# Two layers of graph network on one core: fp32 messages summed unsplit, counting merged with the first sort passes, node stages cut finer

## The chip, the cores and the metric

The kernel runs on one core of one Trainium2 chip. The metric is the device time of one execution in microseconds. One launch computes everything.

## What is computed

N = 6250 nodes with 64 features, E = 200,000 directed edges sorted by `dst`, 64 features per edge. Two layers, each on a normalized `x` and each added back to `x`:

```python
h = relu(layernorm(x))
# layer 1: attention over both directions of every edge
gl, gr = (h @ Wl.T)[src], (h @ Wr.T)[dst]           # src, dst: 2 E entries, 4 heads of 16
score = (att * leaky_relu(gl + gr, 0.2)).sum(-1)
alpha = softmax of score over the entries of one src
out = segment_sum(gr * alpha, src)                  # 6250 x 64
x = x + gelu(concat(out, h) @ W1.T + b1) @ W2.T + b2
# layer 2: plain messages
h = relu(layernorm(x))
agg = segment_sum(h[src] + edge_attr_64, dst)       # 6250 x 64
y = relu(agg @ W1 + b1) @ W2 + b2
x = x + batchnorm(y) * gamma + beta
```

Everything is fp32. `src` and `dst` are drawn at random, so each row of `h[src]` is fetched by its index.

## The kernel before, in words

The nodes lie in 49 blocks of 128 (a partition each). Seven stages follow one another, each a block of five instruction lists with a barrier of all engines behind it.

1. `prepare`: first layernorm, the tables `gl_table` and `gr_table` in HBM, and one sort key per entry (block and node numbers in 26 bits, carried as fp32), 3136 of the 4096 columns of `keys`. How many keys lie below each block boundary is counted 49 times over all 3136 columns: 28 times by VectorE (L431), 21 times by ScalarE (L332, sign with a running sum). From the counts come the padding keys in the columns from 3072 on, which make every block's share a multiple of 256. Both engines write the counting's waste into `keys[1]`.
2. `sort`: a bitonic sort of 128 x 4096 keys. Stages 1 to 11 work within runs along a partition: 66 passes over the whole array, of four instructions of 1024 elements each (`one_pass_by_runs`, L538 to L541). Then eight stages that cross partitions, with transposes on TensorE (L610) and copies back on ScalarE (L619). GpSimd's only part is an iota, `bits` (L519), for which the first VectorE instruction waits (L550).
3. `decode`: VectorE unpacks keys into rows and places. The row numbers to gather, `row_of` (L700), are the last but three of its instructions.
4. `attention`: 403 steps of 1024 entries in 13 chunks. GpSimd issues eight indirect gathers of 128 rows a step (L815), in eight slots; VectorE makes one-hots (L970, L1002) and scans scores, TensorE multiplies.
5. `attention_nodes`: dividing by the softmax's sums (`share` L1248, `mixed` L1251), then 13 rounds of at most four blocks on TensorE and ScalarE; VectorE adds each round to `x` (L1259), and when all are in, does the layernorm over all 49 blocks (five operations over 3136 columns); a store of `h2_table` ends it. GpSimd makes `nodes` by an iota, clears `agg`, and copies `dst_f` meanwhile.
6. `messages`: 98 groups of 2048 edges, 196 halves of eight tiles of 128. For each half GpSimd issues eight gathers (L1308) into one of six slots. VectorE adds the edge rows into PSUM (L1384), makes a bf16 one-hot of `dst` (L1358), and together with ScalarE splits the message in three bf16 parts (L1387, L1391), which TensorE sums by one-hots (L1329) in one matmul of 192 columns per tile. A group whose edges span more than one block of nodes takes a step more for each further block, with a one-hot of all 16 tiles made of two SBUF operands, `nodes` and `dst_f` (48 such steps in all).
7. `message_nodes`: the three parts of `agg` are added over all blocks (L1508, L1509), then matmuls, batch norm and the store.

A buffer is reused when the last reader has signalled. The order on each engine is the order in which the code is written; no planner is at work. GpSimd's gathers of a half wait for `s_message` of the half six before.

## Time and profile before

| | us |
|---|---|
| median of 3 runs | 7588.72 (7580.87 to 7643.47) |
| the profiled execution | 7608.22 |
| its span | 7606.3 |
| prepare, to the first pass of the sort | 0 to 172 |
| 66 passes within runs | 172 to 483 |
| crossing stages of the sort | 483 to 1095 |
| decode | 1095 to 1134 |
| attention, gathers | 1134 to 5225 |
| attention's end (last scan and sums) | 5225 to 5371 |
| attention_nodes | 5371 to 5461 |
| messages, gathers | 5461 to 7522 |
| last sums and message_nodes | 7522 to 7606 |

The page's first part gives each engine's busy time over the whole span. Since the stages have different limits, these shares say little of any one stage. The groups by line tell how long an engine was idle just ahead of an instruction, and what ended it. A timeline row is one instruction, or several alike. Idle time that stands before a gather as "issue" is the pause that GpSimd makes between two of them.

### The profile page before, as it was taken

What the parts mean: (1) busy time and instruction counts of PE and PEld (TensorE: products, weight loads), DVE (VectorE), ACT (ScalarE), POOL (GpSimd) and SP (SyncE); (2) the same over time, 40 slices, a digit from 0 to 9 for tenths busy, and PEclk for the clock granted to TensorE, in tenths of its full rate; (3) what the DMA queues carried; (4) which work ended last, traced back from release to release, by engine and by line L of the source; (5) the groups of instructions that cost most, each with busy time, mean ns of one, the idle gap of its engine ahead of it and who ended that gap; (6) DMA issues with size and microseconds to landing.
All of it is one profiled execution on the core that took longest, in us unless ns stands there. A gap on an engine that the chain in (4) does not pass through costs nothing. (4 is left out here: it accounts for less than half of the span.)

```text
span 7606.3 us, 71089 instructions
## 1 busy us (share of the span) xinstructions
PE 3570.6 (47%) x16583; PEld 3314.3 (44%) x16583; DVE 4721.4 (62%) x7539; ACT 733.2 (10%) x1147; POOL 4711.1 (62%) x4809
## 2 busy tenths in 40 slices
PE   2001114476776767677677776767411112222224
PEld 1001114466666767676676666767311111111112
DVE  8999993567676776767667676777433333333443
ACT  4001100000000000000000000000111111111111
POOL 0000007777777777777777777773277777777774
PEclk9995555555555555555555555555655555555555
DMA  2000004344443444444444443442122221111111
GB/s 35 0 0 0 0 20 103 103 120 118 116 118 103 135 115 120 118 113 121 111 127 115 117 122 100 135 112 83 44 51 53 51 51 50 50 50 50 49 47 29
DMA packets 631893, 600.13 MB, mean 79 GB/s; under 512 B 382418, under 2 KB 385618, under 8 KB 631206
## 3 DMA queue, kind: packets, MB, share of 16 engines
q10 hardware_dynamic: 177888, 320.64, 12.9%
q0 software_dynamic: 153344, 157.33, 10.4%
q1 hardware_dynamic: 300230, 117.47, 5.9%
q8 instruction: 142, 2.33, 0.1%
q14 instruction: 289, 2.37, 0.1%
HBM read 480.76 MB, written 114.19 MB: 78 GB/s over the span
## 5 line engine op out<-in xcount | busy, mean ns | idle before, releaser
L815 POOL DMA_INDIRECT rows<-gr_table,row_of x3224 | 3109.2, 964 | 1946.2 <-issue 1945.0
L1308 POOL DMA_INDIRECT message<-h_table,src_sb x1568 | 1582.8, 1009 | 552.7 <-issue 477.6
L846 PE MATMUL bank<-terms,hot_sum 128*128 128x68 f32 x6448 | 1468.3, 423 | 777.8 <-DVE acc L981 774.2
L846 PEld LDWEIGHTS bank<-terms,hot_sum 128*128 128x128 f32 x6448 | 1409.4, 331 | 826.2 <-DVE hot_sum L1002 820.1
L836 PE MATMUL bank<-gl_step,hot_t 128*128 128x64 f32 x6448 | 1459.1, 421 | 282.4 <-DVE hot_t L970 240.6
L836 PEld LDWEIGHTS bank<-gl_step,hot_t 128*128 128x128 f32 x6448 | 1421.6, 333 | 293.7 <-DVE hot_t L970 290.6
L1329 PE MATMUL bank<-edge_parts,edge_hot 128*128 128x192 bf16 x1568 | 286.3, 364 | 1597.0 <-DVE edge_parts L1391 1597.0
L1022 DVE TENSOR_TENSOR fore<-bank,rows 128x512 f32<-128x512 f32 x403 | 277.7, 689 | 1083.3 <-DMA rows<-gr_table,row_of 1083.3
L1329 PEld LDWEIGHTS bank<-edge_parts,edge_hot 128*128 128x128 bf16 x1568 | 202.6, 140 | 1680.5 <-DVE edge_parts L1391 1669.4
L1384 DVE TENSOR_TENSOR bank<-message,edge 128x512 f32<-128x512 f32 x196 | 142.0, 724 | 1007.1 <-DMA message<-h_table,src_sb 1007.1
L952 ACT ACTIVATE bank<-fore 128x512 f32<-128x512 f32 x403 | 242.4, 602 | 3383.6 <-DVE fore L1022 3383.6
L1002 DVE TENSOR_TENSOR hot_sum<-bank,place 128x1024 f32<-128x1024 f32 x403 | 490.6, 1217 | 0.0
L970 DVE TENSOR_TENSOR hot_t<-place_b,bank 128x1024 f32<-128x1024 bf16 x403 | 489.2, 1214 | 0.7 <-DMA place_b<-place_rows 0.7
L981 DVE TENSOR_TENSOR acc<-acc,bank 128x68 f32 x1612 | 354.2, 220 | 182.9 <-DVE acc L981 133.9
L610 PE MATMUL bank<-ident,keys 128*128 128x128 f32 x448 | 96.8, 406 | 787.3 <-DVEq L596 698.8
L610 PEld LDWEIGHTS bank<-ident,keys 128*128 128x128 f32 x448 | 87.1, 217 | 797.8 <-DVEq L596 704.9
L138 DVE TENSOR_REDUCE scores<-top 128x32 f32<-128x512 f32 x403 | 276.3, 686 | 59.5 <-DVE top L1039 1.5
L1028 DVE TENSOR_TENSOR fore<-fore,bank 128x512 f32<-128x512 f32 x403 | 274.5, 681 | 21.3 <-ACT bank L952 21.3
L530 DVE TENSOR_TENSOR keys<-keys 128x1024 f32<-128x1024 f32 (+1 forms) x166 | 275.9, 1662 | 7.9 <-ACT keys L619 2.0
L995 DVE TENSOR_TENSOR terms<-rows_again,bank 128x512 f32<-128x512 f32 x403 | 273.2, 678 | 4.3
L531 DVE TENSOR_TENSOR keys<-keys 128x1024 f32<-128x1024 f32 (+1 forms) x166 | 274.8, 1655 | 0.0
L1039 DVE TENSOR_TENSOR top<-fore,bank 128x512 f32<-128x512 f32 x403 | 273.8, 679 | 0.0
(264 smaller groups left out, 2867.6 us busy)
## 6 DMA issues: line engine op xcount, KB each, us to landing
place_b<-place_rows ACTq DMA_DIRECT2D x403, 256.0 KB, 3.6
gr_rows<-rows ACTq DMA_DIRECT2D x403, 256.0 KB, 2.0
rows_again<-gr_rows ACTq DMA_DIRECT2D x403, 256.0 KB
rows<-gr_table,row_of POOLq DMA_INDIRECT x3224
gl_step<-gl_table SPq DMA_DIRECT2D x1612, 32.0 KB
edge<-in_edge_attr SPq DMA_DIRECT2D x97, 512.0 KB, 3.6
message<-h_table,src_sb POOLq DMA_INDIRECT x1568, 2.4
pen_s<-pen_rows ACTq DMA_DIRECT2D x52, 64.0 KB, 2.0
```

What stands on the lines that cost most here:

```text
L138: return dve.tensor_reduce(out, in_, AX.X, op)
L530: dve.tensor_tensor(vb[:, 0], va[:, 0], va[:, 1], ALU.min)
L531: c.link(dve.tensor_tensor(vb[:, 1], va[:, 0], va[:, 1], ALU.max))
L815: pool.indirect_dma_start(rows[k][:, g, :], None, m.gr_table[:, :], bass.IndirectOffsetOnAxis(m.row_of[:, tile:tile + 1], 0)).then_inc(s_g ...
L836: last = pe.matmul(bank[q % LAG][:, g * D:(g + 1) * D], hot_t[q % LAG][:, g * P:(g + 1) * P], gl_s[q % U][:, g // GROUP_TILES, :], start=T ...
L846: last = pe.matmul(sums_of(r % SUM_SLOTS, g // GROUP_TILES), hot2[r % LAG][:, g, :], by_tile[:, g, :], start=g % GROUP_TILES == 0, stop=g ...
L970: dve.tensor_tensor(hot_t[q % LAG][:, :], place_b[q % V][:, :], node_ps.to_broadcast([P, STEP]), ALU.is_equal).then_inc(s_hot, 1)
L981: dve.tensor_tensor(sums, sums, sums_of(r % SUM_SLOTS, i), ALU.add).then_inc(s_acc, 1)
L1002: dve.tensor_tensor(hot2[r % LAG][:, :, :], places, at, ALU.is_equal).then_inc(s_summed, 1)
L1022: dve.tensor_tensor(z[:, :, :], left_of(q % LAG), rows[q % U][:, :, :], ALU.add).then_inc(s_z, 1)
L1308: pool.indirect_dma_start(rows[k][:, e, :], None, m.h2_table[:, :], bass.IndirectOffsetOnAxis(m.src[:, tile:tile + 1], 0)).then_inc(s_gath ...
L1329: done = pe.matmul(out[:, 0:3 * D], one_hot[:, e, :], parts[h % 4][:, e, :, :].rearrange("p w f -> p (w f)"), start=first and e == 0, stop ...
```

## The change

Six edits:

- **Messages.** ScalarE copies the edge attributes into PSUM, VectorE adds the gathered rows to them into SBUF as fp32, and TensorE sums with fp32 one-hots, 64 columns per tile. No splitting; `agg` is one part, not three. One-hots of the next group are made once this group's messages are. The further one-hot reads its node numbers from PSUM, where a copy of 128 columns puts them.
- **Counting and sorting.** ScalarE does all 49 counts. Meanwhile VectorE runs the sort's stages 1 to 9 on columns 0 to 3071 and stage 10 on the first half; the rest is done once the padding keys stand. `sort` has no block of its own any more; its iota is the second instruction of GpSimd's list.
- **Early gathers.** `row_of` is computed ahead of nine other instructions of `decode`, and GpSimd issues the gathers of the first four steps (32 of 3224) inside `decode`.
- **attention_nodes.** GpSimd's iota, clearing and copy wait for `mixed`. `mixed` is made in two pieces (8 and 41 blocks). The layernorm's mean, difference, square and sum are taken round by round. The last operation and the store are in two pieces (24 and 25 blocks).
- **message_nodes.** The two additions over `agg` are gone.

```diff
-            for b in range(VECTOR_COUNTS, BLOCKS):
-                at_least(act, s_cnt_act, b - VECTOR_COUNTS)
-                nc.scalar.activation(junk_act, src_f[:, :], ACT.Sign, bias=bias[:, b:b + 1],
+            for b in range(BLOCKS):
+                at_least(act, s_cnt_act, b)
+                nc.scalar.activation(junk[:, :], src_f[:, :], ACT.Sign, bias=bias[:, b:b + 1],
                                      accum_out=below[:, b:b + 1]).then_inc(s_cnt_act, 1)
+            sort.scalar(act)
...
+            dve.wait_ge(s_cnt_act, BLOCKS)
+            c.link(dve.tensor_scalar(below[:, :], below[:, :], -0.5, float(EDGE_COLS), ALU.mult, ALU.add))
+            dve.engine_nop().then_inc(s_cnt, 1)
...
+    def vector_front(self, dve):
+        self.c = Chain(dve, self.s_chain)
+        self.stages(dve, 1, self.FRONT_STAGES - 1, 0, self.FRONT)
+        self.stages(dve, self.FRONT_STAGES, self.FRONT_STAGES, 0, ROW // 2)
...
+        self.stages(dve, 1, 7, self.FRONT, self.PADS)
+        self.stages(dve, 8, self.FRONT_STAGES - 1, self.FRONT, ROW - self.FRONT)
+        self.stages(dve, self.FRONT_STAGES, self.FRONT_STAGES, ROW // 2, ROW // 2)
+        self.stages(dve, self.FRONT_STAGES + 1, LOG_ROW - 1, 0, ROW)
```

```diff
+        @block.gpsimd
+        def _(pool):
+            pool.wait_ge(s_row, 1)
+            for q in range(EARLY):
+                for g in range(STEP_TILES):
+                    tile = q * STEP_TILES + g
+                    pool.indirect_dma_start(m.rows[q][:, g, :], None, m.gr_table[:, :],
+                                            bass.IndirectOffsetOnAxis(m.row_of[:, tile:tile + 1], 0)
+                                            ).then_inc(m.s_gath[q], 16)
...
+            dve.wait_ge(s_moved, 8)
+            c.link(dve.tensor_scalar(pad_row[:, :], m.iota_node[:, 0:1], float(BLOCKS * P), None, ALU.add))
+            c.link(dve.tensor_single_scalar(pad_t[:, :], key_t[:, :].bitcast(I32), NODE_MASK, ALU.bitwise_and))
+            dve.tensor_scalar(m.row_of[:, :], pad_t[:, :], pad_row[:, :], None, ALU.min).then_inc(s_row, 1)
...
-            for q in range(STEPS):
+            for q in range(EARLY, STEPS):
```

```diff
+            pool.wait_ge(s_mixed, 2)
...
-                dve.tensor_tensor(m.x[:, b:b + n, :], m.x[:, b:b + n, :],
-                                  bank[4 + r % 2][:, 0:n * D].rearrange("p (b f) -> p b f", f=D), ALU.add
+                x, h, square = (tile[:, b:b + n, :] for tile in (m.x, m.h, mixed))
...
-            layernorm_steps(m, chain, dve, m.x, m.h, mixed, s_var, s_std, 1).then_inc(s_h2, 1)
+                dve.wait_ge(s_add, r + 1)
+                chain.link(nc_reduce(dve, mean, x))
+                chain.link(dve.tensor_scalar(mean, mean, 1.0 / D, None, ALU.mult))
+                chain.link(dve.tensor_tensor(h, x, mean.unsqueeze(2).to_broadcast([P, n, D]), ALU.subtract))
+                chain.link(dve.tensor_tensor(square, h, h, ALU.mult))
+                chain.link(nc_reduce(dve, var, square))
+            dve.tensor_scalar(m.var[:, :], m.var[:, :], 1.0 / D, LN_EPS, ALU.mult, ALU.add).then_inc(s_var, 1)
+            dve.wait_ge(s_std, 1)
+            chain.link(dve.reciprocal(m.rstd[:, :], m.rstd[:, :]))
+            chain.link(dve.tensor_tensor(m.mean[:, :], m.rstd[:, :], m.rstd[:, :], ALU.mult))
+            chain.link(dve.tensor_tensor(m.mean[:, :], m.mean[:, :], m.var[:, :], ALU.mult))
...
+            chain.link(dve.tensor_tensor(m.rstd[:, :], m.rstd[:, :], m.mean[:, :], ALU.mult))
+            for lo, hi in ((0, FRONT), (FRONT, BLOCKS)):
+                h = m.h[:, lo:hi, :]
+                dve.scalar_tensor_tensor(h, h, 0.0, m.rstd[:, lo:hi].unsqueeze(2).to_broadcast([P, hi - lo, D]), ALU.max,
+                                         ALU.mult).then_inc(s_h2, 1)
```

```diff
-    hot = [sb(f"edge_hot{k}", [P, HALF, P], BF16, ctx) for k in range(4)]
-    hot_more = sb("edge_hot_more", [P, 2, HALF, P], BF16, ctx)
-    parts = [sb(f"edge_parts{k}", [P, HALF, 3, D], BF16, ctx) for k in range(4)]
+    rows = [sb(f"edge_rows{k}", [P, HALF, D], F32, ctx) for k in range(U)]
+    edge = [sb(f"edge{k}", [P, 2, HALF, D], F32, ctx) for k in range(W)]
+    messages_s = [sb(f"message{k}", [P, 2, HALF, D], F32, ctx) for k in range(V)]
+    hot = [sb(f"edge_hot{k}", [P, HALF, P], F32, ctx) for k in range(4)]
+    hot_more = sb("edge_hot_more", [P, EDGE_TILES, P], F32, ctx)
+    numbers_ps, past_ps = (bank[3][:, i * P:(i + 1) * P] for i in range(2))
...
-            def scatter(out, one_hot, h, first, last):
+            def scatter(out, one_hot, g, way, first, last):
                 for e in range(HALF):
-                    done = pe.matmul(out[:, 0:3 * D], one_hot[:, e, :], parts[h % 4][:, e, :, :].rearrange("p w f -> p (w f)"),
...
             for h in range(HALVES):
-                act.wait_ge(s_message, h + 1)
-                nc.scalar.copy(parts[h % 4][:, :, 0, :], message_of(h)).then_inc(s_hi, 1)
-                act.wait_ge(s_rest, h + 1)
-                nc.scalar.copy(parts[h % 4][:, :, 1, :], message_of(h)).then_inc(s_mid, 1)
+                g, way = h // 2, h % 2
+                act.wait_ge(s_edge[g % W], (g // W + 1) * 16)
+                at_least(act, s_message, h - 1)
+                nc.scalar.copy(edge_ps(h), edge[g % W][:, way, :, :]).then_inc(s_edge_ps, 1)
...
+            def hot_first(g):
+                for h in (2 * g, 2 * g + 1):
+                    hot_of(hot[h % 4][:, :, :], numbers_ps, m.dst_f[:, h * HALF:(h + 1) * HALF], HALF
+                           ).then_inc(s_hot_first, 1)
...
+            hot_first(0)
             before = steps_before(dve, 0)
             for g in range(EDGE_GROUPS):
                 for way in range(2):
                     h = 2 * g + way
-                    k = h % U
-                    message, piece = message_of(h), parts[h % 4]
-                    dve.wait_ge(s_edge[g % V], (g // V + 1) * 16)
-                    dve.wait_ge(s_gath[k], (h // U + 1) * 16 * HALF)
-                    dve.tensor_tensor(message, rows[k][:, :, :], edge[g % V][:, way, :, :], ALU.add).then_inc(s_message, 1)
-                    hot_of(hot[h % 4][:, :, :], bank[3][:, 0:P], m.dst_f[:, h * HALF:(h + 1) * HALF], HALF)
-                    dve.wait_ge(s_hi, h + 1)
-                    dve.tensor_tensor(message, message, piece[:, :, 0, :], ALU.subtract).then_inc(s_rest, 1)
+                    dve.wait_ge(s_edge_ps, h + 1)
+                    dve.wait_ge(s_gath[h % U], (h // U + 1) * 16 * HALF)
+                    dve.tensor_tensor(messages_s[g % V][:, way, :, :], edge_ps(h), rows[h % U][:, :, :], ALU.add
+                                      ).then_inc(s_message, 1)
                     if g and not way:
                         add_first(g - 1, before)
-                    dve.wait_ge(s_mid, h + 1)
-                    dve.tensor_tensor(piece[:, :, 2, :], message, piece[:, :, 1, :], ALU.subtract).then_inc(s_parts, 1)
+                if g + 1 < EDGE_GROUPS:
+                    hot_first(g + 1)
...
-                        hot_of(hot_more[:, :, :, :].rearrange("p a t n -> p (a t) n"), m.nodes[:, bass.ds(past * P, P)],
-                               m.dst_f[:, g * EDGE_TILES:(g + 1) * EDGE_TILES], EDGE_TILES).then_inc(s_hot, 1)
+                        dve.tensor_copy(past_ps, m.nodes[:, bass.ds(past * P, P)]).then_inc(s_past, 1)
+                        dve.wait_ge(s_past, r + 1)
+                        hot_of(hot_more[:, :, :], past_ps, m.dst_f[:, g * EDGE_TILES:(g + 1) * EDGE_TILES], EDGE_TILES
+                               ).then_inc(s_hot, 1)
...
             c = Chain(dve, s_chain)
-            c.link(dve.tensor_tensor(m.agg[:, :, 1, :], m.agg[:, :, 1, :], m.agg[:, :, 2, :], ALU.add))
```

VectorE in `messages`, before: one half and the start of the next. `edge_parts` are the bf16 parts, `edge` the attributes, `message` the gathered rows (and, in the bank, their sum).

```order
L1384 TENSOR_TENSOR bank<-message,edge 128x512 [waits s_edge_gath2,s_edge1]
L1358 TENSOR_TENSOR edge_hot<-bank,dst_f 128x1024
L1387 TENSOR_TENSOR bank<-bank,edge_parts 128x512 [waits s_edge_hi]
L1363 TENSOR_LOAD first_of
L1363 ISA x2
L1365 REGISTER_ALU
L1367 ISA [waits s_edge_first_ps,s_agg]
L1367 TENSOR_TENSOR agg<-agg,bank 128x192
L1391 TENSOR_TENSOR edge_parts<-bank,edge_parts 128x8x64 [waits s_edge_mid]
L1384 TENSOR_TENSOR bank<-message,edge 128x512 [waits s_edge_gath3,s_edge1]
L1358 TENSOR_TENSOR edge_hot<-bank,dst_f 128x1024
L1387 TENSOR_TENSOR bank<-bank,edge_parts 128x512 [waits s_edge_hi]
```

And now, a half and the next, then the one-hots of the next group; `edge_rows` are the gathered rows.

```order
L1454 TENSOR_TENSOR message<-bank,edge_rows 128x512 [waits s_edge_gath2,s_edge_attr_ps]
L1434 TENSOR_LOAD first_of
L1434 ISA x2
L1436 REGISTER_ALU
L1438 ISA [waits s_edge_first_ps,s_agg]
L1438 TENSOR_TENSOR agg<-agg,bank 128x64
L1454 TENSOR_TENSOR message<-bank,edge_rows 128x512 [waits s_edge_gath3,s_edge_attr_ps]
L1423 TENSOR_TENSOR edge_hot<-bank,dst_f 128x1024 x2
```

The first addition had two inputs in SBUF; it has one in PSUM now. Per half two subtractions are gone, and both one-hots of a group come together behind its additions.

GpSimd from the last instruction of `prepare` to the gathers, before (the ISA without a name ahead of the iota is no arithmetic).

```order
L353 ISA spans<-span 128x196 [waits s_span]
L285 UNCONDITIONAL_BRANCH
L517 UNCONDITIONAL_BRANCH [waits barrier_Pool_Activation_PE_DVE_SP_gather]
L519 ISA
L519 IOTA bits 128x7
L516 UNCONDITIONAL_BRANCH
L806 UNCONDITIONAL_BRANCH [waits barrier_Pool_Activation_PE_DVE_SP_gather]
L815 DMA rows<-gr_table,row_of 128x64 x64
```

And now.

```order
L353 ISA spans<-span 128x196 [waits s_span]
L283 UNCONDITIONAL_BRANCH
L690 UNCONDITIONAL_BRANCH [waits barrier_Pool_Activation_PE_DVE_SP_gather]
L696 DMA rows<-gr_table,row_of 128x64 [waits s_dec_row]
L696 DMA rows<-gr_table,row_of 128x64 x31
L679 UNCONDITIONAL_BRANCH
L846 UNCONDITIONAL_BRANCH [waits barrier_Pool_Activation_PE_DVE_SP_gather]
L855 DMA rows<-gr_table,row_of 128x64 x32
```

The iota `bits` has moved to the start of `prepare`, behind the clearing of `ident`, and half of the 64 gathers in sight have moved ahead of a barrier, to where `s_dec_row` releases them.

## Rows read from the trace of the kernel before

**Rows 1.** The page's first part: busy time, share of the span, instructions of each engine.

```profile
PE 3570.6 (47%) x16583; PEld 3314.3 (44%) x16583; DVE 4721.4 (62%) x7539; ACT 733.2 (10%) x1147; POOL 4711.1 (62%) x4809
```

**Rows 2.** Groups of instructions, message stage: busy us, mean ns | idle before, releaser.

```profile
L1308 POOL DMA_INDIRECT message<-h_table,src_sb x1568 | 1582.8, 1009 | 552.7 <-issue 477.6 <-POOLq L1161 75.1
...
L1384 DVE TENSOR_TENSOR bank<-message,edge 128x512 f32<-128x512 f32 x196 | 142.0, 724 | 1007.1 <-DMA message<-h_table,src_sb 1007.1
```

**Rows 3.** One line's instructions: duration ns min/median/max, first and last start.

```profile
L815 POOL DMA_INDIRECT rows<-gr_table,row_of x3224: 940/944/2982, 1133.8 to 5224.4; - x190
L1308 POOL DMA_INDIRECT message<-h_table,src_sb x1568: 940/944/2864, 5461.2 to 7520.6; - x196
```

**Rows 4.** Timeline, message stage: start us, duration us, engine, line, operation [idle before].

```profile
6511.57 0.70 DVE L1384 TENSOR_TENSOR bank<-message,edge 128x512 f32<-128x512 f32 x1 [6.08 <-DMA message<-h_table,src_sb]
6511.67 1.41 POOL L1308 DMA_INDIRECT message<-h_table,src_sb  x1 [0.30 <-issue]
...
6516.22 2.29 DVE L1358 TENSOR_TENSOR edge_hot_more<-nodes,dst_f 128x2048 bf16<-128x2048 f32 x1 [0.87 <-issue]
...
6517.12 2.20 POOL L1308 DMA_INDIRECT message<-h_table,src_sb  x1 [0.31 <-issue]
```

**Rows 5.** Timeline, attention stage.

```profile
2502.85 1.22 DVE L1002 TENSOR_TENSOR hot_sum<-bank,place 128x1024 f32<-128x1024 f32 x1
2503.02 0.94 POOL L815 DMA_INDIRECT rows<-gr_table,row_of  x1 [0.30 <-issue]
```

**Rows 6.** Timeline, prepare and sort.

```profile
46.44 3.41 DVE L431 TENSOR_SCALAR_CACHE_REDUCE keys<-src_f 128x3136 bf16<-128x3136 f32 x1
...
80.44 2.92 ACT L332 ACTIVATE keys<-src_f,bias 128x3136 bf16<-128x3136 f32 x1
...
144.23 0.18 DVE L434 TENSOR_SCALAR below<-below 128x21 f32<-128x21 f32 x1 [0.88 <-ACT keys L332]
...
160.75 0.99 DVE L490 CAST blk_i<-blk_f 1x1612 int32<-1x1612 f32 x1
...
169.99 1.28 DVE L550 TENSOR_SCALAR bits<-bits 128x1 int32<-128x1 int32 x7 [8.25 <-POOL bits L519]
...
189.09 1.23 DVE L539 TENSOR_TENSOR keys<-keys 128x1024 f32<-128x1024 f32 x1
...
193.75 1.23 DVE L539 TENSOR_TENSOR keys<-keys 128x1024 f32<-128x1024 f32 x1
...
1042.31 0.68 DVE L581 TENSOR_TENSOR keys<-keys 128x512 f32<-128x512 f32 x1
...
1042.91 0.69 DVE L580 TENSOR_TENSOR keys<-keys 128x512 f32<-128x512 f32 x1
```

**Rows 7.** Timeline, end of decode and first gather of the attention stage.

```profile
1123.18 1.91 DVE L700 TENSOR_SCALAR row_of<-seg_i,pad_row 128x3232 int32<-128x3232 int32 x1
...
1133.75 1.29 POOL L815 DMA_INDIRECT rows<-gr_table,row_of  x1 [963.80 <-issue]
```

**Rows 8.** Busy time in one window, decode: start:end, length, busy us (instructions), PEclk, DMA share, GB/s.

```profile
1102.80:1132.50 29.70, 29.08 (x13) 0.53 0.17 71
```

**Rows 9.** Timeline, one gather while VectorE scans a chunk.

```profile
1464.88 2.37 POOL L815 DMA_INDIRECT rows<-gr_table,row_of  x1 [0.30 <-issue]
```

**Rows 10.** Timeline, node stage after attention.

```profile
5371.12 5.39 DVE L1248 TENSOR_SCALAR share<-acc 128x196 f32<-128x196 f32 x1
...
5381.44 0.42 PE L1185 MATMUL bank<-ident,mixed 128*64 128x128 f32 x1 [17.01 <-DVE mixed L1251]
...
5425.67 0.42 DVE L1259 TENSOR_TENSOR x_sb<-x_sb,bank 128x256 f32<-128x256 f32 x1 [3.46 <-PE bank L1204]
...
5431.09 3.42 DVE L138 TENSOR_REDUCE mean<-x_sb 128x49 f32<-128x3136 f32 x1
...
5461.16 2.15 POOL L1308 DMA_INDIRECT message<-h_table,src_sb  x1 [75.10 <-POOLq L1161]
```

**Rows 11.** Timeline, start of the last node stage.

```profile
7536.39 1.91 PE L1442 MATMUL bank<-ident,agg 128*64 128x128 f32 x8 [7.83 <-DVE agg L1509]
```

More of the change, by code:

```diff
@@ L194, in build @@
         m.row_of = sb("row_of", [P, TILES_UP], I32, layer0)
+        m.rows = [sb(f"rows{k}", [P, STEP_TILES, D], F32, layer0) for k in range(GATHER_SLOTS)]
+        m.s_gath = [sem(f"s_gath{k}") for k in range(GATHER_SLOTS)]
         m.keys = [sb("keys0", [P, ROW], F32, keys_ctx), sb("keys1", [P, ROW], F32, keys_ctx)]
         with ExitStack() as ctx:
-            prepare(m, ctx)
-        if stop == "prepare":
-            return m
-        with ExitStack() as ctx:
-            final = sort(m, ctx)
+            final = prepare(m, ctx, Sort(m, ctx))
         if stop == "sort":
@@ L227, in build, with prepare @@
         return m
-def prepare(m, ctx):
+def prepare(m, ctx, sort):
     nc, t, sb, sem, bank = m.nc, m.t, m.sb, m.sem, m.bank
@@ L716, in attention @@
     PAIRS = STEP_TILES * HEADS
-    rows = [sb(f"rows{k}", [P, STEP_TILES, D], F32, ctx) for k in range(U)]
+    rows = m.rows
     rows2 = [sb(f"rows_again{k}", [P, STEP_TILES, D], F32, ctx) for k in range(V)]
@@ L752, in attention @@
     s_pool = m.s_pool
[L753 removed]
+    s_gath = m.s_gath
     s_store = [sem(f"s_store{k}") for k in range(U)]
```

337 lines of the change are left out of this document (177 added, 160 removed).

## The prediction, made before the changed kernel ran

> **What bounds the kernel now.** I read the page's first part to see whether one engine fills the span. None does: TensorE 47%, VectorE and GpSimd 62% each [rows 1]. So each stage has its own limit, and I went through the stages.
>
> The two gather stages hold 6150 of 7606 us. In `messages` VectorE's addition L1384 stood idle 1007 us ahead of itself, waiting for gathered rows [rows 2]. The gathers wait for nobody: ahead of them GpSimd's idle time is "issue" (477.6 us over 1568) and the one stage change (75.1) [rows 2]. So this stage is as long as GpSimd needs to issue 1568 gathers: 2060.4 us from 5461.2 to the end of the last at 7521.5 [rows 3]. VectorE, TensorE and ScalarE there matter only by what they do to GpSimd.
>
> They do something. The median gather takes 944 ns, the mean 1009 [rows 2, 3]. The timeline shows which are the long ones: one issued just after L1384 (two inputs in SBUF) takes 1.41 us, one under L1358 with `nodes` and `dst_f` in SBUF 2.20 us; each ends about 0.8 us after the VectorE instruction does [rows 4]. In the attention stage the one-hot L1002 (one input in PSUM) runs 1.22 us and the gather beside it takes 0.94 [rows 5]. There only scans, with long instructions that read SBUF alone, hold gathers up [rows 9]. So an instruction with two SBUF inputs holds the next gather until its end, and one with an input in PSUM doesn't. The undisturbed pace is 0.944 + 0.305 (the pause, 477.6/1568) = 1.249 us.
>
> Outside the gather stages VectorE sets the pace: in `prepare` and `sort` it stands still 8.25 us for the iota `bits` [rows 6] and otherwise hardly at all.
>
> **Messages: 101 us gained.** All of VectorE's instructions over a half now have an input in PSUM: the addition, the one-hots, the sums, and the further one-hot, which gets its numbers by a copy of 128 columns. The kind of L1002 [rows 5] then holds for every one. The excess of the gathers is 1582.8 − 1568 × 0.944 = 102.6 us [rows 2, 3]; the stage becomes 1568 × 1.249 = 1958, plus 1 for its first gather (2.15 [rows 10]), so 1959 against 2060.4. Do others become the bound? A half lasts 8 × 1.249 = 10.0 us. VectorE has about 0.7 + 1.22 [rows 2, 5] and a small sum per half, 2.5 us; TensorE eight fp32 matmuls, at most 3.4 if each takes 0.42 as a 128-column one does [rows 10]; ScalarE has one copy where it had two. A further step adds 16 matmuls and 2.3 us of VectorE, 48 times in all. Six slots of rows cover that. Bounds: 80, if the SBUF to PSUM copy and other short accesses still hold some; 103, if nothing does.
>
> **Prepare and sort: 105 us gained.** VectorE gives up 28 counts, 46.44 to 144.2, about 97 us [rows 6]. Every sort pass it does ahead of the counts' end is work it must do anyway. Its price: an instruction of 1024 elements comes every 1.135 us, four make 4.66 with the pass's 0.12 [rows 6]; 512 elements take 0.60 [rows 6]. So one takes 0.07 + 1.04 ns per element. Stages 1 to 9 are 45 passes of 768: 45 × 3.6 = 162; ten passes of 512 are 25; with 2 for the start the front is 189, from 46.4 to 236. ScalarE's 49 counts at 3.04 each (21 of them fill 80.44 to 144.2) last from 80.4 to 229 [rows 6], 7 us ahead of VectorE. Behind come 21 us of small operations (as before, 144.2 to 161.7 [rows 6], with the round trips), then the pads: 28 passes of 64 elements at about 0.66, 19; stages 8 and 9 on the 1024 other columns, 17 × 1.46 = 25; stage 10 on the second half, 25; stage 11 in full, 11 × 4.66 = 51; 2 for the bits. End: 236 + 21 + 120 = 377, against 483 before (172 + 66 × 4.66 + 3). The sort itself is no shorter (309 for 311); the gain is the counts and the 8.25 us gap, whose iota now runs at the very start. That the iota costs 8 us there is hidden by the loads of `prepare`. Bounds: 85, if the small pad instructions take twice my figure (nothing as short as 64 elements with this pattern is in my rows); 108 if VectorE waits for nothing at all. ScalarE becomes the later one if a count takes over 0.14 us more than it did.
>
> **Early gathers: 9 us gained.** Now the first gather starts at 1133.75, behind the block's end [rows 7]; the 33rd comes 32 × 1.249 = 40 us later, 1173.7. In the changed order `row_of` is ready after the three moved instructions, at 1106.9 in the old times, and VectorE's other nine end at 1132.1: the 29.1 us busy of the window less the 3.9 of the moved ones is 25.2 [rows 8]. Several have two SBUF inputs. For those that have one (tensor_scalar over 4096 columns) no gather of before shows what they do. If all eight long ones hold a gather each, 8 are out at 1132.1, and 24 × 1.249 = 30 later all 32; with 1.4 for the stage change the 33rd starts at 1163.5: 10 gained. If none holds, it starts at 1148.4: 25 gained. I take 9, nearest the first end, since a scan's instructions hold gathers for 2.37 us too [rows 9]. The low end is 0: the barrier behind `decode` must now wait for GpSimd, and a start-up of 7 to 8 us on GpSimd, like the gap ahead of `bits`, could lie before the first.
>
> Here the Trainium skill speaks: "SBUF — State Buffer" says that `tensor_scalar` with fp32 in SBUF can enter a mode that takes the port pair shared with GpSimd, for the whole instruction. By that rule the gain would be 10, without it up to 25; no trace here shows it.
>
> **attention_nodes: 19 us gained.** `share` takes 5.39 us for 196 elements, of which 0.3 is work; GpSimd's iota lies beside it [rows 10]. Since that waits now for `mixed`, and TensorE needs only 8 of 49 blocks (0.6 for 3.4 us), TensorE starts about 7.7 earlier than 5381.44 [rows 10]. VectorE adds a round every 3.46 + 0.42 = 3.88 us [rows 10]; the five operations for 256 columns, at 3.42 per 3136 [rows 10], fill some 2.4 of these with starts and links, so they are hidden. Behind the last round four operations of 3.42 become those of one round and of one block, 3.4 in all: 10.3. The split last operation and store bring 1.5. Together 19.5, I take 19. What is late next is TensorE's 13 rounds, unchanged. Bounds 12 to 22: its clock stood at 0.50 when it started and rose on the way; a start at another moment can shift the rise by some us.
>
> **Last sums and nodes: 9 us gained.** TensorE waited 7.83 us for the two additions over `agg` [rows 11]; they are gone, 6.9. The last half has no subtractions: 2. Bounds 1 to 10.
>
> Attention keeps its 3224 gathers, its scans and its pace; I cost it at nothing. The smaller `agg` clearing is hidden as before.
>
> **Sum.** 101 + 105 + 9 + 19 + 9 = 243 us, against the profiled execution's 7608: 7365. That execution is 19.5 above the median of the three runs, 7588.7, so the forecast as a median is 7346, said as **7347**.
>
> **Rivals.**
>
> *The pace of the message stage stays.* If the long gathers come from something else (the edge attributes' transfers, say), the 101 are lost: 7448. Against it: rows 4 show them just under these two instructions, and rows 5 none. 0.06.
>
> *The front of the sort is dearer.* ScalarE's counts beside VectorE's passes slow down, or the pad passes cost double: up to 40 us, 7387. Its counts ran beside VectorE's before too, at 3.04 [rows 6]. 0.07.
>
> *Early gathers unhindered.* With GpSimd issuing at its own pace under `decode`'s one-input instructions, 16 more: 7331. 0.05. *Early gathers for nothing*, the 9 lost: 7356, 0.04.
>
> *Slower.* PSUM inputs don't help, and GpSimd is held by every fp32 instruction that writes SBUF. In each half it would stand 0.70 + 1.22 us, in each of the 48 further steps 2.29: 196 × 1.92 + 110 = 486 us, instead of 102.6 before. With the other 142 gained it comes out at +241, 7830. It decides from 243/196 = 1.25 us held per half on, over today's. The attention stage, whose instructions are of this kind and whose median gather is 944 ns [rows 3, 5], speaks against it: 0.01.
>
> My forecast has 0.77. The range that leaves out no more than 2 in 10 is **7320 to 7390**: the sums of the bounds taken together would be wider (187 to 268 gained), but they won't all fall on one side; it takes in the dear front, both cases of the early gathers and the drift of 20 us between runs. One per cent, 76 us, is about what a measurement of this kernel (63 us between its slowest and fastest run) can tell from no change. Faster by over 1%: 0.97, within 1%: 0.02, slower by over 1%: 0.01.
>
> **What will show it.** Of `messages`: mean gather near 0.945 instead of 1.009 us, 1959 us from first to last, no gather of 1.4 us by the addition. Of sort: the first pass of the sort proper with all 4096 keys' last stage ends near 377. Of `decode`: gathers under its last nine instructions, one by one with each, and the stage's end at 1163 less 105. Of the node stage: `share` at 0.3, TensorE 3 us after the stage's start, 71 us where 90 were. Of the end: no `agg` over 49 blocks. I would be wrong if the mean gather stays at 1.0, or if a further step of TensorE (16 fp32 matmuls, 48 times) empties the slots and the gathers wait for `s_message`.

## The result: 7363 us, 3% faster, and the profile after

| | before | after |
|---|---|---|
| median, us | 7585.01 (7580.87 to 7643.47, 4 runs) | 7363.48 (7360.45 to 7367.2, 4 runs) |
| ratio | | 0.9686, 95% interval 0.9645 to 0.9727 |
| profiled execution, span | 7606.3 | 7362.5 |

The forecast was 7347, range 7320 to 7390. Against the profiled execution it was 7365; that execution took 7364.5 (its span and 2 us around it). The traced execution of the kernel before took 7608.22, 23 us above the median of its four runs here, and the changed kernel's 1 us above its own. So the two traces differ by 243.8 us, the medians by 221.5.

The page after, its first part, and the groups of the two gather stages (columns as in [rows 1] and [rows 2]):

```profile
PE 4204.2 (57%) x18919; PEld 4018.0 (55%) x18919; DVE 4363.1 (59%) x7419; ACT 702.3 (10%) x1007; POOL 4625.4 (63%) x4809
...
L855 POOL DMA_INDIRECT rows<-gr_table,row_of x3192 | 3075.4, 963 | 976.4 <-issue 970.8
...
L1371 POOL DMA_INDIRECT edge_rows<-h_table,src_sb x1568 | 1480.8, 944 | 531.4 <-issue 477.5
...
L1454 DVE TENSOR_TENSOR message<-bank,edge_rows 128x512 f32<-128x512 f32 x196 | 135.5, 692 | 1071.3 <-DMA edge_rows<-h_table,src_sb 1068.6
...
L696 POOL DMA_INDIRECT rows<-gr_table,row_of x32 | 50.1, 1567 | 958.5 <-DVE row_of L727 949.0
```

TensorE and GpSimd hold a larger share of a shorter span, which says nothing by itself. What answers to [rows 2] is the third line: the mean message gather takes 944 ns, as the median does, with 477.5 us of pauses as before. VectorE still stands idle for gathered rows. First and last start of that line's gathers (columns as in [rows 3]), and a stretch of the timeline with the same two kinds of instruction as in [rows 4]:

```profile
L1371 POOL DMA_INDIRECT edge_rows<-h_table,src_sb x1568: 940/944/2327, 5329.5 to 7286.9; - x196
```

```profile
6390.77 0.69 DVE L1454 TENSOR_TENSOR message<-bank,edge_rows 128x512 f32<-128x512 f32 x1 [8.88 <-DMA edge_rows<-h_table,src_sb]
...
6391.94 0.94 POOL L1371 DMA_INDIRECT edge_rows<-h_table,src_sb  x1 [0.31 <-issue]
...
6393.96 2.29 DVE L1423 TENSOR_TENSOR edge_hot_more<-bank,dst_f 128x2048 f32<-128x2048 f32 x1
6394.43 0.94 POOL L1371 DMA_INDIRECT edge_rows<-h_table,src_sb  x1 [0.30 <-issue]
6395.68 0.94 POOL L1371 DMA_INDIRECT edge_rows<-h_table,src_sb  x1 [0.30 <-issue]
```

Under the 2.29 us of the further one-hot, now with `bank` in place of `nodes`, two gathers pass at 0.94 us each.

The difference of the two traces by stage follows. Each stage is cut at the same instruction of both; the columns sum to the spans.

| stage, from what to what | before, us | after, us | gained | forecast |
|---|---|---|---|---|
| prepare and sort, to decode's first unpacking | 1095.9 | 990.4 | 105.5 | 105 |
| decode, to the start of the 33rd gather | 78.2 | 75.2 | 3.0 | 9 |
| attention, 33rd to last gather | 4050.3 | 4047.1 | 3.2 | 0 |
| attention's end, to `share` | 146.7 | 145.8 | 0.9 | 0 |
| attention_nodes, to the first message gather | 90.0 | 71.0 | 19.0 | 19 |
| messages, first to last gather | 2059.4 | 1957.4 | 102.0 | 101 |
| last sums and message_nodes | 85.7 | 75.6 | 10.1 | 9 |
| sum | 7606.3 | 7362.5 | 243.8 | 243 |

### The profile page after: what moved, and what is told of

It reads as the page before. It is cut to its first block and busy times, and to the rows that moved or that the text cites. A ratio compares the mean times of both kernels' runs of the same rounds, so it can differ in the third digit from the quotient of the medians.

```text
span 7362.5 us, 75948 instructions
## 1 busy us (share of the span) xinstructions
PE 4204.2 (57%) x18919; PEld 4018.0 (55%) x18919; DVE 4363.1 (59%) x7419; ACT 702.3 (10%) x1007; POOL 4625.4 (63%) x4809
## 5 line engine op out<-in xcount | busy, mean ns | idle before, releaser
L1371 POOL DMA_INDIRECT edge_rows<-h_table,src_sb x1568 | 1480.8, 944 | 531.4 <-issue 477.5
L1392 PE MATMUL bank<-message,edge_hot 128*128 128x64 f32 x3136 | 714.6, 423 | 877.4 <-DVE message L1454 877.4
L1392 PEld LDWEIGHTS bank<-message,edge_hot 128*128 128x128 f32 x3136 | 683.5, 330 | 908.5 <-issue 908.5
L1454 DVE TENSOR_TENSOR message<-bank,edge_rows 128x512 f32<-128x512 f32 x196 | 135.5, 692 | 1071.3 <-DMA edge_rows<-h_table,src_sb 1068.6
L1392 PE MATMUL bank<-message,edge_hot_more 128*128 128x64 f32 x1536 | 340.3, 423 | 50.4 <-DVE edge_hot_more L1423 50.4
L1392 PEld LDWEIGHTS bank<-message,edge_hot_more 128*128 128x128 f32 x1536 | 331.2, 332 | 59.4 <-DVE edge_hot_more L1423 59.4
L1417 ACT COPY bank<-edge 128x512 f32<-128x512 f32 x196 | 115.4, 589 | 1839.9 <-DVE message L1454 1823.2
```

Of the source, the lines that this page charges most:

```text
L1371: pool.indirect_dma_start(rows[h % U][:, e, :], None, m.h2_table[:, :], bass.IndirectOffsetOnAxis(m.src[:, tile:tile + 1], 0)).then_inc(s_ ...
L1392: done = pe.matmul(out[:, 0:D], one_hot[:, e, :], messages_s[g % V][:, way, e, :], start=first and e == 0, stop=last and e == HALF - 1)
```

## The experiments

My theory: a gather is held (lasts longer than 0.94 us) when VectorE, at its start, runs an instruction that reads both inputs from SBUF; what the other stages gained is VectorE's time there, or a wait of VectorE's that went. The rivals: the smaller work of unsplit sums; gathers that are held by any long instruction; for the sort, the counts' move alone. The runs fall into three groups, each on a chip of its own with the kernel before beside it: add_sbuf to iota_first; early0 to scan_both with after_again; front_behind, iota_free, norm_whole and warm_nodes. Medians are compared within a group. Where a stage is compared, it is by the profiles, one for each kernel.

### Which edit of the message stage gave the 102 us

**add_sbuf**: the addition reads two SBUF operands again. (SyncE's reload of `edge` must then wait for the addition too, which the cut leaves out.)

```diff
-dve.tensor_tensor(messages_s[g % V][:, way, :, :], edge_ps(h), rows[h % U][:, :, :], ALU.add
+dve.tensor_tensor(messages_s[g % V][:, way, :, :], edge[g % W][:, way, :, :], rows[h % U][:, :, :], ALU.add
```

> The changed kernel, but VectorE adds two operands in SBUF again (edge attributes and gathered rows); ScalarE's copies stay. Theory (an instruction with two SBUF inputs holds the gather that starts beside it): in the kernel before 51 gathers of 1.3 to 1.6 us carried 25 us of excess, so message gathers take 1983 instead of 1958 us, mean 960 ns, median time 7389. Rival A (every one of the 196 additions holds a gather for 0.47 us): 92 more, 7455. Rival B (inputs do not matter, the unsplit sum did it): 7363.

**more_sbuf**: the further one-hot reads two SBUF operands again.

```diff
-dve.tensor_copy(past_ps, m.nodes[:, bass.ds(past * P, P)]).then_inc(s_past, 1)
-dve.wait_ge(s_past, r + 1)
-hot_of(hot_more[:, :, :], past_ps, ...
+hot_of(hot_more[:, :, :], m.nodes[:, bass.ds(past * P, P)], ...
```

> The changed kernel, but the further one-hots read their node numbers from SBUF, without the copy into PSUM. Theory: the 48 instructions of about 2.3 us with two SBUF inputs hold a gather each; before, 47 gathers of 2.0 to 2.9 us carried 76 us of excess, so the stage becomes 2034 us and the median 7440. Rival B (inputs do not matter): 7363.

**split_psum**: the kernel before, splitting and all, with the operands' places changed and the copies added that this takes.

```diff
 # ScalarE, a half ahead of its splitting
+act.wait_ge(s_edge[g % V], (g // V + 1) * 16)
+at_least(act, s_parts, h)
+nc.scalar.copy(message_of(h + 1), edge[g % V][:, way, :, :]).then_inc(s_edge_ps, 1)
 # VectorE
-dve.tensor_tensor(message, rows[k][:, :, :], edge[g % V][:, way, :, :], ALU.add)
+dve.tensor_tensor(message, message, rows[k][:, :, :], ALU.add)
+dve.tensor_copy(past_ps, m.nodes[:, bass.ds(past * P, P)]).then_inc(s_past, 1)
-hot_of(hot_more[...], m.nodes[:, bass.ds(past * P, P)], ...
+hot_of(hot_more[...], past_ps, ...
```

> The kernel before, with its three bf16 parts, its 192-column matmuls and three sums per block, but with the edge attributes copied into PSUM by ScalarE ahead of the addition, and the further one-hot fed from PSUM. Theory (operand place alone): mean gather 944 ns, message gathers 1958 us, median 7585 - 101 = 7484. Rival B (less work per half on VectorE, ScalarE and TensorE did it): 7585. In between, both share.

Medians: add_sbuf 7384.05, more_sbuf 7435.41, split_psum 7513.65, beside 7604.62 for the kernel before; ratios 0.9702 (0.9673 to 0.9732), 0.9784 (0.9744 to 0.9823), 0.9871 (0.9842 to 0.9901). The message gathers in the profiles, in this order:

```profile
L1371 POOL DMA_INDIRECT edge_rows<-h_table,src_sb x1568: 940/944/2325, 5329.4 to 7296.7; - x196
```

```profile
L1371 POOL DMA_INDIRECT edge_rows<-h_table,src_sb x1568: 941/947/2386, 5338.2 to 7360.9; - x196
```

```profile
L1310 POOL DMA_INDIRECT message<-h_table,src_sb x1568: 940/944/2157, 5496.9 to 7454.1; - x196
```

First to last, 1967.3, 2022.7 and 1957.2 us. The last settles it: with the operands' places changed, and all the splitting kept, the stage takes what it takes after the change (1957.4). The unsplit sum is worth nothing there. Rival B falls; rival A too, by add_sbuf's +10 where it asked for 92.

My sizes for the two parts were too large: +10 for 25 expected, +65 for 76 (5 of these 65 are the pace: this profile's median gather takes 947 ns). I counted the gathers over 1.2 us that overlap the instruction. In the kernel before there are 51 beside the addition (25.2 us over 944 ns each) and 48 beside the further one-hot (77.0); in add_sbuf 19 beside the addition (9.1), in more_sbuf 48 beside the further one-hot (62.1).

The count differs between executions of the same code too. iota_first (below) has the message stage of the kernel before unchanged, and in its trace only 18 gathers beside the addition are long (9.1 us), with 48 beside the further one-hot (83.4). Its message gathers, source view as above:

```profile
L1307 POOL DMA_INDIRECT message<-h_table,src_sb x1568: 940/947/2853, 5454.6 to 7507.8; - x196
```

First to last these are 2053.2 us at a median of 947 ns, against 1961.2 in after_again at the same 947: a gain of 92, where the pair of traces at 944 gives 102. So the size of this gain varies by some 10 us with the execution, and the medians agree with the lower end: split_psum lies 91.0 below the kernel before.

What varies can be seen in the kernel before. Two additions, each with the gather that starts next:

```profile
6481.15 0.70 DVE L1384 TENSOR_TENSOR bank<-message,edge 128x512 f32<-128x512 f32 x1 [1.49 <-DMA message<-h_table,src_sb]
6481.20 1.45 POOL L1308 DMA_INDIRECT message<-h_table,src_sb  x1 [0.30 <-issue]
...
6595.06 0.77 DVE L1384 TENSOR_TENSOR bank<-message,edge 128x512 f32<-128x512 f32 x1 [6.14 <-DMA message<-h_table,src_sb]
6595.10 0.94 POOL L1308 DMA_INDIRECT message<-h_table,src_sb  x1 [0.30 <-issue]
```

In this trace the 51 held gathers start 0.045 to 0.13 us behind the start of the addition; the 129 that start from 0.047 us ahead of it to 0.042 behind it take 0.94 us. The addition starts when the last rows of its half have landed, so a few hundredths of a microsecond decide. That is also why the two shares don't add up to 102 when put back one at a time.

### Prepare and sort

**iota_first**: the kernel before, with the iota `bits` moved to the second place of GpSimd's list.

```diff
 pool.memset(m.ident[:, :], 0.0).then_inc(s_ident, 1)
+pool.iota(m.bits[:, :], [[0, LOG_P]], base=0, channel_multiplier=1).then_inc(m.s_num, 1)
```

> The kernel before, with the iota of the sort's bits as the second instruction of GpSimd in the first stage instead of the first of the sort. Theory: the 8.25 us that VectorE stood ahead of the sort go, and nothing takes their place: 7577, sort starting 8 us earlier. Rival: GpSimd's start-up lies on the path at the stage's end wherever the iota is, or delays the constants of the first stage: 7585.

**front_behind**: the changed kernel, no sort pass ahead of the counts' end.

```diff
-sort.vector_front(dve)
+sort.c = Chain(dve, sort.s_chain)
 # in vector_rest
-self.stages(dve, 1, 7, self.FRONT, self.PADS)
-self.stages(dve, 8, self.FRONT_STAGES - 1, self.FRONT, ROW - self.FRONT)
-self.stages(dve, self.FRONT_STAGES, self.FRONT_STAGES, ROW // 2, ROW // 2)
-self.stages(dve, self.FRONT_STAGES + 1, LOG_ROW - 1, 0, ROW)
+self.stages(dve, 1, LOG_ROW - 1, 0, ROW)
```

> The changed kernel, with all 49 counts on ScalarE but no sort pass ahead of their end. Theory: VectorE waits from 46 to 229, then does all 66 passes of 4.66 us: the first 11 stages end at 229 + 24 + 309 = 562 instead of 375, +187, that is 80 us slower than before in this part: it is the passes beside the counts that gain, not the counts' move. Rival: ScalarE's 49 counts run faster without VectorE's passes beside them (under 2.9 us each), +150.

iota_first: decode starts at 1087.2, 8.7 us earlier than in the kernel before: the gap is gone, as expected. The median of ten runs, 7595.77 beside 7604.62, cannot tell it (ratio 0.9995, 0.9975 to 1.0014); nine of the ten took 7586.7 to 7635.2, one took 9432.74, and no trace shows why. Its profile shows something I had not looked for; it comes below with `share`.

front_behind: median 7548.42 beside 7598.56 (0.9928, 0.99 to 0.9956). Its decode starts at 1170.0, 179.6 later than after the change and 74 later than before. (Three of its eight runs took some 39 us more than the other five; the profiled run, 7585.32, is one of them, and in it TensorE's clock stood at 0.50 through the node stage; see the end of this document.) ScalarE's last count, and VectorE's first sort pass:

```profile
226.12 2.91 ACT L330 ACTIVATE acc<-src_f,bias 128x3136 bf16<-128x3136 f32 x1
...
244.02 2.01 DVE L552 TENSOR_TENSOR keys<-keys 128x1024 f32<-128x1024 f32 x1
```

A count lasts 2.91 us without passes beside it, and 2.91 with them in the changed kernel: the passes don't slow ScalarE, and the rival falls. The 7 us by which I overestimated are the small operations, which VectorE had done while it waited. So the counts' move without the passes costs 74 us although the moved iota is in it too, some 83 without that; the passes beside the counts make of it a gain of 105, 8.7 of it the iota's. What the passes did slow is GpSimd: its all-reduce takes 6.53 us in the changed kernel, 0.94 before and 0.95 in front_behind. Its result isn't needed before 236, so this costs nothing. In the changed kernel VectorE ends the front at 236.3, where I had 236, and the small pad passes show the 0.14 us for 64 elements that I had extended from longer ones:

```profile
236.26 0.21 DVE L434 TENSOR_SCALAR low_i<-spans 128x98 int32<-128x98 f32 x1
...
239.79 0.19 DVE L453 TENSOR_SCALAR below<-below 128x49 f32<-128x49 f32 x1
240.79 0.21 DVE L456 COPY counts<-bank 128x49 f32<-128x49 f32 x1 [0.81 <-PE bank L381]
...
258.11 0.23 DVE L552 TENSOR_TENSOR keys<-keys 128x64 f32<-128x64 f32 x1
258.25 0.22 DVE L553 TENSOR_TENSOR keys<-keys 128x64 f32<-128x64 f32 x1
...
374.95 1.28 DVE L584 TENSOR_SCALAR bits<-bits 128x1 int32<-128x1 int32 x7
```

VectorE needs no wait for ScalarE at 239.79 (the 0.81 behind it is TensorE's sum), and the bits follow at 374.95 on the last pass, with no gap.

### Early gathers

**early0**: no early gathers.

```diff
-EARLY = 4
+EARLY = 0
```

> The changed kernel with no gather in the decode stage (EARLY = 0), row numbers still made early. Theory, by the trace of the changed kernel (five gathers issued under eight long instructions, and 3.85 us from the last early gather to the first of the next stage): the 33rd gather comes 3 us later, total +3. The forecast as I made it (a gain of 9): +9. The rival without holding: +25.

In the changed kernel, VectorE and GpSimd in decode:

```profile
1001.80 4.42 DVE L728 SCALAR_TENSOR_TENSOR seg<-seg_i,keys 128x4096 f32<-128x4096 int32 x1
1002.19 6.36 POOL L696 DMA_INDIRECT rows<-gr_table,row_of  x1 [949.01 <-DVE row_of L727]
1006.13 2.29 DVE L729 TENSOR_SCALAR seg_i<-seg_i 128x4096 int32<-128x4096 int32 x1
...
1008.45 4.43 DVE L730 SCALAR_TENSOR_TENSOR place_r<-keys,seg_i 128x4096 bf16<-128x4096 f32 x1
1008.85 4.86 POOL L696 DMA_INDIRECT rows<-gr_table,row_of  x1 [0.30 <-issue]
...
1019.96 1.84 DVE L741 TENSOR_SCALAR place<-pad_t 128x3232 f32<-128x3232 int32 x1
1020.35 3.45 POOL L696 DMA_INDIRECT rows<-gr_table,row_of  x1 [0.30 <-issue]
1021.84 1.84 DVE L742 TENSOR_SCALAR keys<-key_t 128x3232 int32<-128x3232 int32 x1
...
1060.82 0.94 POOL L696 DMA_INDIRECT rows<-gr_table,row_of  x1 [0.30 <-issue]
...
1065.62 0.94 POOL L855 DMA_INDIRECT rows<-gr_table,row_of  x1 [3.85 <-POOLq L679]
```

The first gather is held through a two-input instruction and the tensor_scalar behind it (1002.19 to 1008.55), the fourth (1020.35) through two tensor_scalars with one input each. So tensor_scalars from SBUF to SBUF hold gathers too, as "SBUF — State Buffer" of the Trainium skill, section "Who interferes with whom", had it: by that rule the rival with 25 us falls, and this trace agrees. But where I let one gather through per instruction, a gather meets a second one before it is done: five pass under eight instructions. Behind an instruction with two inputs the gather still needs some 0.8 us (1012.88 to 1013.71), and a tensor_scalar that starts in this time holds it once more; behind the tensor_scalar it ends within 0.13 us (1008.42 to 1008.55). And the step to the next stage costs 3.85 us behind a gather where I had 1.4, the step behind VectorE before. In early0 the 33rd gather starts 78.5 us behind decode's start, in the changed kernel 75.2: the early gathers bring 3.3 us, as expected from the trace. The median of early0, 7407.19, is 35 us above after_again's; that is not theirs but TensorE's clock in the node stage (at the end of this document): that stage is 110.6 us long there, and three of the four runs took 7405.9 to 7408.8. Its fastest run took 7368.08, after_again's two fastest 7365.5 and 7365.78.

### The node stage

**iota_free** and **norm_whole**: the changed kernel, with one of its edits in `attention_nodes` undone each.

```diff
 # iota_free
-pool.wait_ge(s_mixed, 2)
```

```diff
 # norm_whole: inside the loop over rounds before, behind it and over all blocks now
-chain.link(nc_reduce(dve, mean, x))
...
+x, h, square, mean, var, n = m.x[:, :, :], m.h[:, :, :], mixed[:, :, :], m.mean[:, :], m.var[:, :], BLOCKS
+chain.link(nc_reduce(dve, mean, x))
```

> The changed kernel, with GpSimd's iota, clearing and copy in the node stage waiting for nothing. Theory: share takes 5.4 us again instead of 0.3, TensorE starts 5 us later, +5. Rival: the wait for x or for the rounds covers it, 0.

> The changed kernel, with mean, difference, square and sum of the layernorm over all 49 blocks behind the last round again. Theory: four operations of 3.42 us come back and the tail of one round goes: node stage 81 instead of 71 us, +10. Rival: the per-round operations delayed the rounds, so +5 or less.

iota_free: median 7366.01, and four of its five runs between 7362.4 and 7367.9, where the changed kernel had 7360.5 to 7367.2 in the result. TensorE starts 2.5 us behind `share`, as in the changed kernel. My explanation of `share` falls. VectorE and GpSimd at the stage's start, in iota_free and in iota_first:

```profile
5261.61 0.30 DVE L1294 TENSOR_SCALAR share<-acc 128x196 f32<-128x196 f32 x1
...
5268.45 5.36 POOL L1205 IOTA nodes<- 128x6272 f32 x1 [150.31 <-issue]
```

```profile
5369.88 0.29 DVE L1247 TENSOR_SCALAR share<-acc 128x196 f32<-128x196 f32 x1
...
5376.72 5.36 POOL L1163 IOTA nodes<- 128x6272 f32 x1 [152.25 <-issue]
```

In both `share` takes 0.3 us though nothing makes the iota of `nodes` wait for it, and in both the iota starts 6.8 us behind `share`; in the kernel before it starts 0.1 us ahead of it. In the order of instructions, GpSimd's list has the nameless ISA once ahead of the first iota that follows the all-reduce of `prepare`: before the change that is `bits` (the 8.25 us in front of the sort), in the changed kernel, iota_free and iota_first it is `nodes`. So a start-up of about 7 us lies once between the ISA and that iota, in front of the sort or in the node stage. That the all-reduce makes it necessary is my reading of the order; no run leaves the all-reduce out. Moving `bits` gained its gap in front of the sort, and by delaying `nodes` also the 5.1 us of `share`; the wait for `mixed` is worth nothing that a run shows. iota_first has both (its node stage takes 84.7 us for 90.0).

norm_whole: median 7377.5; its node stage takes 80.6 us for 71.0, +9.6 for +10 expected. The rival (+5 or less) falls: the per-round layernorm is hidden behind TensorE, as costed.

**after_again**: the changed kernel on the chip of early0, scan_psum and scan_both.

> The changed kernel once more, as the measure for the others of this call. About 241 us below the kernel before on the same chip; message gathers 1957 us if the median gather takes 944 ns, 5 more if it takes 947; the node stage 71 us, or some 36 more if TensorE's granted clock stays at 0.50 through it.

Median 7371.87 (7365.5 to 7402.19) beside 7627.62 (7588.29 to 7633.36). Its profile has gathers of 947 ns and a message stage of 1961.2 us, a span of 7376.0. The 13.5 us between the changed kernel's two profiles are mostly this pace: 3 ns by 4792 gathers are 14 us.

### A faster version, from the same rule

The trace after still shows 63 us of held gathers in attention, all beside the scans: 29.3 beside the first pair and its end, 33.4 beside the second and the maximum. **scan_psum** lets the first pair read scores where TensorE left them; **scan_both** has ScalarE put the scores back for the second.

```diff
 # scan_psum; the reverse scan likewise
-chain.link(dve.tensor_tensor_scan(fore[:, :], pen_s[:, 0:SCAN], score_s[:, :], -BIG, ALU.add, ALU.max))
+chain.link(dve.tensor_tensor_scan(fore[:, lo], pen_s[:, lo], scan_bank(0)[:, :], -BIG, ALU.add, ALU.max))
+chain.link(dve.tensor_tensor_scan(fore[:, hi], pen_s[:, hi], scan_bank(1)[:, :], fore[:, mid - 1:mid], ALU.add, ALU.max))
```

```diff
 # scan_both, ScalarE; VectorE signals s_free_ps when a bank has been read, and scans it again
+act.wait_ge(s_free_ps, 2 * c + i + 1)
+nc.scalar.copy(scan_bank(i)[:, :], score_s[:, i * HALF * P:(i + 1) * HALF * P]).then_inc(s_again_ps, 1)
```

> The changed kernel, with the first two scans of each chunk of attention cut in halves that read their scores in PSUM instead of SBUF. Theory: the 29 us of excess of the 24 gathers beside them go, the 33 us beside the second pair and the maximum stay; total -29. Rival (a scan holds gathers wherever its operand lies, or the four shorter scans hold as much): 0 or a few us more.

> As the one before, and ScalarE copies the scores back into PSUM so that the second pair of scans and the subtraction read them there too; only the maximum of two SBUF arrays is left (13 times 1.2 us). Theory: of 62 us of excess about 10 are left; total -50 against the changed kernel. Rival: the chain of a chunk grows by the copies, the slots fill, and gathers wait: a gain under 30.

scan_psum: 7337.5 (0.9656, 0.961 to 0.9702). scan_both: 7311.09 (0.9621, 0.9574 to 0.9669). The fastest runs, 7336.43 and 7308.54, are 29 and 57 below after_again's 7365.5. From the 33rd to the last gather attention takes 4016.0 and 3987.1 us, where the changed kernel took 4047.1: 31 and 60 less. Behind the last gather the longer chain of scans and copies takes 148.9 and 153.6 us for 145.8, so 3 and 8 come back. The spans are 28.0 and 52.3 shorter than the changed kernel's, for 29 and 50 expected in total. Gathers beside the scans in scan_both:

```profile
L856 POOL DMA_INDIRECT rows<-gr_table,row_of x3192: 940/944/1950, 1064.7 to 5051.8; - x200
```

```profile
1365.98 1.28 DVE L1144 TENSOR_TENSOR_SCAN fore<-pen_s,init,bank 128x512 f32<-128x512 bf16 x1 [0.71 <-ACT bank L981]
1366.77 0.94 POOL L856 DMA_INDIRECT rows<-gr_table,row_of  x1 [0.30 <-issue]
...
1371.75 1.53 POOL L856 DMA_INDIRECT rows<-gr_table,row_of  x1 [0.30 <-issue]
```

Only the maximum of two SBUF arrays still holds a gather now and then: in six of the 12 chunks one takes 1.21 to 1.95 us (the 1.53 here), 3.4 us over 944 ns each in all. The stage is at GpSimd's pace: 3191 pauses and gathers at 1.249 us are 3986. This version beats both kernels, and nothing that I ran is clearly faster; the next measures the same.

**warm_nodes**: scan_both with 12 transposes at the start of TensorE's node stage that nobody reads.

```diff
+for i in range(12):
+    pe.transpose(bank[2][:, i % 4 * P:(i % 4 + 1) * P], m.ident[:, :], m.ident[:, :])
```

> The version with both pairs of scans fed from PSUM, and TensorE starts the node stage after attention with 12 transposes that nobody reads, while it would otherwise wait for the first piece of mixed. Two of ten profiles so far had TensorE's granted clock at 0.50 through this stage (36 us longer), the others rose to 1.00 some 3 us after its start. Theory A: the clock rises 2 to 3 us earlier, about -2 us, and how often it fails stays as it was (one run in four or so 37 us slower). Theory B: activity ahead decides whether it rises, so the failing runs vanish. Rival: no effect, or a later start by 1 us.

Median 7313.85 (7311.61 to 7314.5, 6 runs; 0.9609, 0.958 to 0.9637). Its node stage took 70.8 us in the profile, scan_both's 71.5. No time is gained. None of its six runs was some 40 us slower, of scan_both's four one was; that is too few to call theory B shown. The granted clock rose 5.5 us behind `share` in its profile, and 5.4 to 7.2 behind it in the seven other profiles of changed kernels in which it rose, so theory A isn't shown either.

## Why the prediction was right, step by step

- **Messages, 101 for 102.0.** The mechanism held, and split_psum shows it alone. The size held for this pair of traces; iota_first and after_again, and the median of split_psum, give 91 to 92, so that it came out at 102.0 is partly luck. What I could not see from the trace before was the share of each instruction, and I gave none; my later shares (25 and 76) were too large when put back one at a time.
- **Prepare and sort, 105 for 105.5.** The front ended at 236.3 (236), the counts at 229 (229), the bits came at 375 (377). The "2 for the bits" stand in the list but not in the sum of 377, which is the bits' start; with them it is 379, and the bits ended at 376.2. The pitch of 0.07 us + 1.04 ns per element, taken from 512 and 1024, held for 64. That the iota's 8 us would be "hidden by the loads of `prepare`" was wrong: there it takes 0.14 us at 1.25, and the start-up went to `nodes`.
- **Early gathers, 9 for 3.0.** The failed step is "all eight long ones hold a gather each" with "1.4 for the stage change": five gathers passed, not eight, and the change took 3.85 us. Both lay in the stated bounds (0 to 25). That tensor_scalars hold gathers was right.
- **attention_nodes, 19 for 19.0, partly by a wrong cause.** "Since that waits now for `mixed`" is not why `share` fell to 0.3: iota_free shows that it does so without this wait, and iota_first that the moved iota `bits` does it, through the start-up that now lies ahead of `nodes`. The right number for `share` was luck. I had counted the move as worth 8.25 us; it is worth 13. The layernorm's 10 us are shown by norm_whole. The bound of 12 to 22 was too narrow: with TensorE's clock at 0.50 throughout, the stage takes 110.6 us.
- **End, 9 for 10.1.** No sum over 49 blocks is left. split_psum, which keeps the two additions and the three parts, takes 83.8 us there, and so does iota_first, which is the kernel before's in this stage: about 8 are the unsplit sums', the other 2 vary from run to run. The 2 that I gave to the last half's subtractions are not shown.
- **Sum, 243 for 243.8.** The 6 us too much for early gathers were made up by attention, which I had at nothing (3.2 between the gathers, 0.9 behind them), and by 1 more each in messages and at the end. That is luck. split_psum, whose attention is the kernel before's, took 4047.2 between the gathers, and kernels with the changed one's took 4047.1 to 4050.7 at the same 944 ns (the last norm_whole), so nothing shows these 3.2 to be a gain.
- **The rivals.** The pace that stays, the dear front, and the slower one (PSUM inputs that hold too) are refuted by the 1957.4 us and by the pad passes; unhindered early gathers by the rows above. "Early gathers for nothing" lay nearer to the measured 3.0 than my 9 did.
- **The bounds.** Taken together they would give 178 to 268, not 187: 80 + 85 + 0 + 12 + 1. The stated range does not hang on it.
- **The median.** 7347 for 7363.48: the working by the profiled executions was 0.5 us off. I had subtracted the 19.5 us by which the profiled run of before lay above its median, as if the changed kernel's would too; that one lay 1 us above its own. So the gain by medians was forecast at 241.7 and came out at 221.5. By the traces of before and iota_first (102.6 and 91.6 us of held message gathers) some 10 of the difference, an estimate, are held gathers of that one trace; the rest stays open.

## What to carry to other kernels

Where indirect gathers issued by GpSimd are the bound, look at which gathers are longer than the median and what VectorE runs beside them: one operand in PSUM was enough to free them, be the instruction 0.7 or 2.3 us long, and the copy that puts it there paid for itself (92 to 102 us in one stage, 52 in the other). Starting gathers under SBUF-to-SBUF work of VectorE brought little, 3.3 us for 32 of them. And work whose inputs are ready can stand beside a wait, if it must be done anyway: the counts' move without it costs 74 us, with it gains 105. A stage's gain read from one pair of traces carries what varies between executions, here 10 us in 100.

## What was not expected of the hardware

**TensorE's clock in the node stage.** In 10 of 14 profiles the granted clock rose from 0.50 to 1.00 (1.2 to 2.4 GHz) 3 to 5 us after TensorE's start there; in four (early0, iota_free, front_behind, split_psum) it stayed at 0.50. The stage in the changed kernel and in early0 (start:end, length, PE, PEld, DVE, ACT, POOL busy, PEclk, DMA share, GB/s):

```profile
5258.40:5329.50 71.10, 50.47 (x248) 29.44 (x248) 44.78 (x94) 24.39 (x42) 9.46 (x3) 0.81 0.21 46
```

```profile
5261.80:5372.40 110.60, 90.05 (x248) 46.61 (x248) 42.92 (x94) 24.49 (x42) 9.46 (x3) 0.50 0.14 29
```

The same instructions, 71.1 us at a mean of 0.81, 110.6 at 0.50 (1.2 GHz throughout). Before its first matmul TensorE had stood idle for 9.5 us in both; in the kernel before, where the clock rose, and in split_psum, where it did not, it was 17.0. What decides it stays open. Times some 38 us above the rest occurred in runs of nearly every kernel (7402.19 in after_again, 7630 in the kernel before). The four profiles at 0.50 are all of such longer runs, and none of the ten others is; for the runs without a trace it is not shown.

**GpSimd's pace.** The median gather took 944 ns in eight profiles, 945 in front_behind, iota_free and warm_nodes, 947 in after_again, more_sbuf and iota_first. Over 4792 gathers 3 ns are 14 us, more than several of the edits are worth.

**GpSimd's start-up.** Ahead of the first iota behind the all-reduce GpSimd needs about 7 us, once: in front of the sort before, where VectorE stood 8.25 us for it, and in the node stage once `bits` had moved (6.8 us from `share` to the iota in iota_first and iota_free).
